# Attention over edges on one core: the value product moved ahead of the next step's edge part in VectorE's order

## The reference, cut to what matters

```python
q = (xn @ Wq + bq).reshape(n, H, DH); k = ...; v = ...     # H = 8 heads of DH = 32
ep = ef @ We + be                                           # the edge part, 32 numbers per edge
scores = jnp.einsum('ehd,ehd->eh', q[dst], k[src] + ep[:, None, :]) * scale
scores = scores * ew[:, None]
m = jax.ops.segment_max(scores, dst, num_segments=n)
ex = jnp.exp(scores - m[dst]); s = jax.ops.segment_sum(ex, dst, num_segments=n)
out = jax.ops.segment_sum((ex / s[dst])[:, :, None] * v[src], dst, num_segments=n)
```

## Time and profile before

| | us |
|---|---|
| median of 3 runs | 3198.67 |
| lowest, highest | 3198.60, 3204.85 |
| the profiled execution, its own time | 3203.72 |
| its span in the trace | 3202.0 |
| PE busy in the span | 2325.6 (73%) |
| DVE busy | 2264.5 (71%) |
| ACT busy | 1713.2 (54%) |
| POOL busy | 1806.3 (56%) |

### The profile page before, as it was taken

One profiled execution on the slowest core, in us unless ns is written; L12 is line 12 of the kernel. 1 busy time (PEld: TensorE's weight loads), 2 busy tenths in 40 slices (PEclk: granted clock), 3 DMA queues, 4 the chain that ended last, 5 costly groups with the idle time before them and its releaser, 6 DMA issues. The chain is left out here.

```text
span 3202.0 us, 45709 instructions
## 1 busy us (share of the span) xinstructions
PE 2325.6 (73%) x10126; PEld 1822.5 (57%) x10126; DVE 2264.5 (71%) x3463; ACT 1713.2 (54%) x5134; POOL 1806.3 (56%) x1909
## 2 busy tenths in 40 slices
PE   1799999999999999488881444554454454454698
PEld 0677777777777777377771333343343333343576
DVE  4788888888888888411122777787887787787455
ACT  0777777777777777122221444444444444444466
POOL 4577777777777777300004666666666666666211
PEclk7899999999999999667775677777777777777899
DMA  4322222222222222354453666666666666665100
GB/s 150 110 81 81 81 81 81 81 81 81 81 81 81 81 81 81 74 133 138 135 138 115 178 177 176 173 176 178 179 175 174 178 179 177 179 178 171 38 13 15
DMA packets 152556, 387.70 MB, mean 121 GB/s; under 512 B 48695, under 2 KB 63290, under 8 KB 149594
## 3 DMA queue, kind: packets, MB, share of 16 engines
q0 software_dynamic: 105040, 318.92, 35.0%
q1 hardware_dynamic: 47226, 57.18, 6.7%
q10 hardware_dynamic: 272, 11.42, 1.0%
HBM read 362.08 MB, written 36.72 MB: 125 GB/s over the span
## 5 line engine op out<-in xcount | busy, mean ns | idle before, releaser
L1444 PE MATMUL ps_sum<-kv_e,ident 128*128 128x264 f32 x1536 | 562.7, 543 | 664.1 <-DVE kv_e L1497 630.6
L404 POOL DMA_INDIRECT feat<-in_x_rows,idx x732 | 844.1, 1153 | 260.2 <-issue 258.8
L1329 POOL DMA_INDIRECT kv_e<-kv_rows,edge x768 | 727.0, 947 | 366.9 <-issue 310.3
L436 ACT ACTIVATE vsh<-feat,rec_a 128x256 f32<-128x256 f32 x2172 | 884.4, 494 | 24.2 <-DMA feat<-in_x_rows,idx 24.2
L1444 PEld LDWEIGHTS ps_sum<-kv_e,ident 128*128 128x128 f32 x1536 | 421.0, 282 | 805.6 <-issue 499.2
L480 PE MATMUL ps_a<-msg,hot 128*128 128x257 f32 x1440 | 449.1, 393 | 0.0
L482 PE MATMUL ps_a<-msg,hot 128*128 128x256 f32 x1440 | 428.3, 379 | 0.0
L1465 DVE TENSOR_TENSOR kv_e<-kv_e,ps_query 128x2048 f32<-128x2048 f32 x96 | 219.6, 2287 | 237.6 <-DMA kv_e<-kv_rows,edge 237.6
L484 PE MATMUL ps_a<-msg,hot 128*128 128x192 f32 x1440 | 351.4, 325 | 0.0
L482 PEld LDWEIGHTS ps_a<-msg,hot 128*128 128x128 f32 x1440 | 272.8, 189 | 40.0
L484 PEld LDWEIGHTS ps_a<-msg,hot 128*128 128x128 f32 x1440 | 273.1, 190 | 38.3
(11 more groups left out here) (332 smaller groups left out, 3536.9 us busy)
## 6 DMA issues: line engine op xcount, KB each, us to landing
ef<-in_ef_t SPq DMA_DIRECT2D x42, 512.0 KB, 6.4
kv_e<-kv_rows,edge POOLq DMA_INDIRECT x768, 3.6
feat<-in_x_rows,idx POOLq DMA_INDIRECT x732, 3.0
rows_e<-in_ef_t ACTq DMA_DIRECT2D x1, 11152.0 KB, 39.5
rows_e<-rows SPq DMA_DIRECT2D x41, 272.0 KB, 2.3
kv_rows<-kv SPq DMA_DIRECT2D x20, 256.0 KB, 2.0
emb<-in_emb_t SPq DMA_DIRECT2D x182, 16.0 KB, 1.6
xw<-in_x_rows SPq DMA_DIRECT2D x22, 128.0 KB, 2.1
```

The lines of the kernel that those rows point to most:

```text
L404: pool.indirect_dma_start(out=feat[:, u, c, 0, :, :].rearrange("p a b -> p (a b)"), out_offset=None, in_=g.x_rows, in_offset=bass.Indirect ...
L436: ins = act.activation(vsh[:, u % TURN, c, j, :, :], feat[:, u % TURN, c, 0, :, :], ACT.Copy, scale=rec_a[:, u % 2, c, 1 + j:2 + j])
L1329: pool.indirect_dma_start(out=kv[:, u, s, :], out_offset=None, in_=g.kv_rows, in_offset=bass.IndirectOffsetOnAxis(ap=edge[:, u, s, DH + 1: ...
L1444: mm = pe.matmul(out, g.ident[:], kv[:, u, s, D - HEADS:], start=(s == 0), stop=False, skip_group_check=True)
```

## The change

In the steady loop and in the last lap, `values(k)` stands directly behind `scores(k)`, and `keys(k + 1)` behind both; before, `keys(k + 1)` stood between the two. The first `keys(0)` ahead of the loop stays. No instruction is added or removed, and the other engines' programs are the same.

```diff
                 for u in range(RING):
                     k = t * RING + u
                     scores(k, u)
+                    values(k, u)
                     keys(k + 1, t + (u + 1) // RING, (u + 1) % RING)
-                    values(k, u)
             for u in range(RING):
                 k = whole * RING + u
                 scores(k, u)
+                values(k, u)
                 if u + 1 < RING:
                     keys(k + 1, whole, u + 1)
-                values(k, u)
```

## The result

The changed kernel takes 3363.13 us in the median of 4 runs (3362.2 to 3364.76), against 3199.82 us for the kernel before (4 runs, 3198.6 to 3204.85): 1.0508 times, 95% interval 1.049 to 1.0526. It is 163 us slower. The forecast was 3352, in a range of 3336 to 3371. The profiled executions differ by 3364.76 - 3203.72 = 161.0 us, and their spans by as much (3363.0 against 3202.0). A few executions of the kernel of run 6 fell in a slower state; its median counts them, its ratio leaves them out.

A forecast was written before the change was run, and what follows sets the result against it. Before, the reuse loop of three gather copies bounds the 12.69 us step; after, a VectorE-ScalarE loop of 14.35 us. 157.7 over 95 steps - 4.7 at the end = +153.0; 3203.7 becomes 3356.7, median 3352, range 3336 to 3371.

The forecast's parts named there:

- Which wait takes over: VectorE at L1500: waiting for ScalarE's L1389 replaces the gather wait, 3.4 us a step, some 325 us in all.
- T to the end of L1389: ScalarE, from a step's scores being ready (T, end of L1488) to the sum stored: 6.06 us, carried over unchanged.
- L1500 to L1465: VectorE, from the denominator scaling to the next step's keys: 0.12 us, taken between 0.08 and 0.50.
- The other terms: VectorE: L1465 to the dependent L1472 2.32 us, L1472 to scores ready (end of L1488) 5.70 us.
- The ring: Three gather copies, reused after keys, value product and TensorE's burst: 12.30 us a step before, 10.3 after, no longer holding.
- The end of the stage: Attention stage's end: the last gathers of `x` land earlier relative to the last scores, -4.7 us, bounds 0 and -4.9.
- The rivals: Attention steps: faster, about 3064 us (0.02); little difference, 3190 to 3335 (0.03); gather wait stays, up to 3590 (0.03).
- Break-even: At L1500: the new step equals the old 12.69 us if the sum is stored 4.40 us after the scores.
- the faster rival: At L1500: stored-sum wait doesn't decide, step falls to GpSimd's 11.27 us, 135 us saved, about 3064; chance 0.02.

The follow-up runs named there:

- run 6: Changed kernel, ScalarE's storing of the sum (L1389) moved ahead only of the row numbers; 3313.47 us on the second chip, 1.0005 of the kernel before.
- run 1: Changed kernel with `values` split: value product stays ahead of the keys, stored-sum wait and L1500 go behind them; 3150.77 us, 0.9841 of the kernel before.
- run 2: Changed kernel, stored-sum wait and denominator product moved behind the next step's keys and query product; 3069.37 us, 0.9591 of the kernel before.
- run 3: Changed kernel, VectorE untouched, ScalarE's storing of the sum (L1389) moved directly behind the exponentials; 3115.98 us, 0.9733 of the kernel before.
- run 5: Kernel before, ScalarE's row numbers, then the sum, moved ahead of preparing the next steps; 3278.75 us on the second chip, 0.9927 of the kernel before.
- run 9: Kernel before, value product still behind the keys, stored-sum wait and L1500 moved behind the next query product; 3302.13 us, second chip, 0.994.

## Why the prediction was right

- **Which wait takes over.** Right: L1500 waits 94 times in the window, 321.9 us in all (some 325 forecast), and L1465 never starts ahead of it. Runs 1 to 3 remove that wait in three ways, two on VectorE and one on ScalarE, and each time the loss turns into a gain.
- **T to the end of L1389 carries over.** Right: the mean over 96 steps is 6.05 us after as before, 6.06 was put in.
- **L1500 to L1465.** The only term that was mis-sized: 0.12 was chosen between 0.08 and 0.50, measured are 0.11 for u = 1 and 0.19 to 0.20 for the other two, 0.17 in the mean. That is the difference between 14.35 and 14.40 us a step, 5 us in 95. The two steps with the longer gap are those with the `ISA` instruction of L1461 ahead of L1465, as the orders of u = 0 and u = 2 show it; no run tests that it is the reason.
- **The other terms.** L1465 to L1472 2.32 and L1472 to T 5.71, as forecast.
- **The ring is off the path.** Right: GpSimd waits for TensorE 7.9 us in all, and VectorE for gathers only once.
- **The end of the stage.** -4.7 forecast, -3.6 measured, for two reasons. The last gather of `kv_e` started 17.5 us ahead of T and not 18.7: the edge gather started 0.84 us behind the row numbers, where I had put 0.1; these came 0.3 us later in that step than the 4.9 put in; and the last two steps took 28.5 us and not 28.7. And ScalarE's end, not the landing, may close the stage now: 3148.87 beside a landing near 3148.7, because TensorE's last burst took 6.43 us.
- **The start and the median.** The remaining 3.0 us lie ahead of the stage, in unchanged instructions. Of the 11 us between 3352 and 3363, 5 are the steps, 3 this, 1 the end, less 1 behind it, and 3.4 come from the median: the profiled execution of before lay 5.0 us above it, the changed kernel's only 1.6.
- **The rivals.** Break-even was put at a sum stored 4.40 us behind T. No run tests it cleanly. Run 6 came out level with the kernel before (1.0005), but that is no proof: on its chip the sum came 5.36 us behind T in the mean, and the kernel before took about 100 us more than on the first. What bears the point out are its quickest steps, about 12.6 us with the sum stored near 4.30, beside the 12.69 of the kernel before on the first chip. Run 3, with the sum at 1.1, came near the faster rival's side, though at 11.77 us a step and not 11.27, as there the row numbers are late.

The rule of the Trainium skill (PSUM — Partial Sum Buffer, Engine vs sequencer instructions) that VectorE's queue is strictly first in, first out is borne out: L1465 followed L1500 in all 95 steps.

## What to carry to other kernels

When an instruction is moved ahead, list the waits that move with it and what then queues behind them; a short last instruction of a helper (here 0.17 us) can bring the longest wait. Follow what raises that semaphore back to its own start: if that start is released by the same engine, the move closes a loop, and its length is the new lower limit of a step. Where the trace shows such a loop, split the helper and put its wait where the signal has come already; here that made a loss of 5% a gain of 4%.

## What the runs showed of the hardware

- Where GpSimd stood waiting, it mostly started a gather 0.80 to 0.85 us behind the instruction that released it, whether that was ScalarE (2308.34 to 2309.18 in the changed kernel) or TensorE (2326.81 to 2327.61), while VectorE started 0.15 us behind ScalarE.
- On the second chip the kernel before took 3% to 4% longer than on the first. In the runs there ScalarE stood idle between its own instructions, for up to 7.3 us (in run 5, first line), mostly at irregular places; the list of waits of run 6, 1765 to 2900 us, has such time under "issue":

```profile
2061.22 0.21 ACT L1365 ACTIVATE score<-best 128x8 f32 x1 [7.33 <-issue]
...
ACT short L1354 <- issue: 92.0, 55, 3.9
...
ACT score L1365 <- issue: 50.8, 50, 4.7
```

For L1354 that compares with 29.4 us, at most 0.3 each, in the kernel before in the group of the result. The durations of VectorE's products (2.29 us) and of GpSimd's gathers (0.95 us) were the same. What holds ScalarE up isn't known; no run tests it, and no trace of the kernel before exists from that chip. The orders weren't stretched alike: T to the sum's end was 6.32 us in the median with two copies in the changed order and 7.44 with the same two in the old one, and in run 9, without copies, 8.95, where the same ScalarE program took 6.03 in the kernel before and in runs 1 and 2. Whether the changed order is less exposed because its gathers are further ahead stays open.
